# One wait for four PSUM banks becomes four waits, one at each head's first matmul, in a fused attention and expert block

## The chip, the cores and the metric

The kernel runs on one core of a Trainium2 chip. The metric is the device time of one launch in microseconds (us). The core has five engines with an instruction queue each: TensorE (PE in the profile, with its weight loads shown as PEld), VectorE (DVE), ScalarE (ACT), GpSimd (POOL) and SyncE (SP). They are ordered by semaphores alone.

## The reference, cut to what matters

```python
# x: (8, 512, 256), 16 heads, 64 rope columns and 16 content columns each
h = _layernorm(x, axis=-1) * (1 + ca) + sa
q, k, v = ...                                  # low-rank projections, rope on q_r and k_r
attn = jnp.einsum('bhqd,bhkd->bhqk', q, k) * SCALE
attn = jax.nn.softmax((attn + causal_mask).astype(jnp.float32), axis=-1)
x = x + ga * (einsum('bhqk,bhkd->bhqd', attn, v) @ w_out.T)
h = _layernorm(x, axis=-1) * (1 + cb) + sb
x = x + gb * routed_experts(h)                 # 8 merged experts, silu(gate) * up, down
```

The change touches how `attn` is computed: the raw scores, and the row maxima that the softmax subtracts.

## The kernel before, in words

The eight batch entries are eight blocks of work, one after the other. In this text block 0 is the first and block 7 the last. Each engine gets the same list of steps (`SETUP_ORDER`, `BODY_ORDER`, `LAST_ORDER`), written out by hand, and picks its part of each step. Block 0 is unrolled, blocks 1 to 6 are one loop (`Fori`), block 7 is unrolled with its own list. In the loop, the value that a semaphore is waited for depends on the block, so it has to be computed in a register first; outside it, it is a constant. A step is named by its kind and its indices: `score.021` is the kind `score` for this block (first digit 0; 1 would be the next block), head group 2, piece 1.

There are 16 heads in 4 groups of 4. A group's head h lies on partitions 32h to 32h+31, so that the four heads' matmuls use four separate row strips of TensorE. For each group there are three `maxima` steps and three `score` steps, each a quad of four PSUM banks, one for each head:

- `maxima` (lines 1086 to 1109): one matmul for each head that adds the causal mask (L1095, all 128 rows, 128 or 256 columns), and then three parts (L1104), each with one or two matmuls for each head. VectorE then takes the row maxima bank by bank (`reduce`, L863), and each of its banks is free (`max_read`) when its head is reduced.
- `score` (lines 1114 to 1128): eight parts (L1124), each with one or two matmuls for each head, the heads innermost. ScalarE then takes exponentials bank by bank (`exp`, L672), which frees the bank (`exp_ready`).

All other TensorE results take one bank: `rope` (L981 to L983, rotated by VectorE at L839), `qcon` and `kcon`, `gate`, `up`, and so on. There are seven banks, `ring0` to `ring6`, used in turn: a step's bank is the one that was used seven places earlier, and its first matmul has to wait until that earlier use has been read. `last_use` names the semaphore and the value. `take_banks` (line 387) gathers the waits of several banks, and `wait_latest` keeps for each semaphore only the highest value:

```python
def take_banks(e, b, part, steps, also=()):
    used = [last_use(b, part, step) for step in steps]
    ...
    wait_latest(e, b, [u for u in used if ...] + list(also))
    return [bank(part, PLACES[part][0][step]) for step in steps]
```

A quad calls it once, for its four banks and for its operands (`q_hi`, `rope_hi` and `k_ready` for the first `maxima` of a group; `rope_lo` and `shifted` for the first `score`). What waits there are is put on the instructions that follow: the last on the quad's first weight load, those before it on register instructions, or on instructions that do nothing else.

The other steps that the text speaks of: `value` (L1140) multiplies the exponentials with the values into the eighth bank `av`; `mix` (L1153) is the output projection, `mixed` its residual on VectorE; `qcon_hi` (L664) and `kcon_lo` (L845) make the halves of the content columns; `join` (L966, L969) ends a block on VectorE.

Of the kernel before, what the change touches and what calls it, by code (L numbers as in the profile page):

```python
# [21 lines left out]
HG = 4  # L22
# [142 lines left out]
def block_program(nc, x, wu_t, w_dq, wk_t, wdkv_t, wuk_t, wuv_t, wo_p, gw_t, gup_t, dn_t, groups, chosen,  # L165
# [3 lines left out]
    with ctx:  # L169
# [103 lines left out]
        k_ready = Count(sem("k_ready"), NG)  # L273
        q_lo = Count(sem("q_lo"), NG)
        max_read = Count(sem("max_read"), NG * NMAX * HG)
        shifted = Count(sem("shifted"), NG)
# [27 lines left out]
        waits_passed = sem("waits_passed")  # L304
# [94 lines left out]
        def wait_latest(e, b, wanted):  # L399

            latest = {}
            for count, ahead, k in wanted:
                name = id(count)
                if name not in latest or (ahead, k) > latest[name][1:]:
                    latest[name] = (count, ahead, k)
            for count, ahead, k in latest.values():
                wait(e, count, b, ahead, k)

        def take_banks(e, b, part, steps, also=()):

            used = [last_use(b, part, step) for step in steps]
            for u in used:
                if u in SETUP_READ:
                    e.wait_ge(*SETUP_READ[u])
            wait_latest(e, b, [u for u in used if u is not None and u not in SETUP_READ] + list(also))
            return [bank(part, PLACES[part][0][step]) for step in steps]

        def take_bank(e, b, part, step, also=()):
            return take_banks(e, b, part, [step], also)[0]
# [556 lines left out]
        def _(pe):  # L976
# [26 lines left out]
            def program(pe, b, part, steps):  # L1003
                for step in steps:
# [80 lines left out]
                    elif kind == "maxima":  # L1085


                        g, i = step[2:]
                        places = take_banks(pe, b, part, [(*step, h) for h in range(HG)],
                                            [(q_hi, ahead, g), (rope_hi, ahead, 2 * g + 1), (k_ready, ahead, g)] if i == 0 else ())  # L1090
                        first, span = MAX_JOBS[i][0], MAX_JOBS[i][-1][1] + (MAX_JOBS[i][-1][0] + 1) * P
                        diagonal = slice(first[1] + first[0] * P, span)
                        own = [P, (diagonal.stop - diagonal.start) // P, P]
                        for h in range(HG):
                            pe.matmul(places[h][:, diagonal].rearrange("p (n k) -> p n k", k=P), ident_b[:, :],  # L1095
                                      mask_qk[:, :].unsqueeze(1).broadcast_to(own), start=True, stop=False,
                                      skip_group_check=True)
# [15 lines left out]
                        last.then_inc(full_sem, 1)  # L1113
                    elif kind == "score":
                        g, n = step[2:]
                        places = take_banks(pe, b, part, [(*step, h) for h in range(HG)],
                                            [(rope_lo, ahead, 2 * g + 1), (shifted, ahead, g)] if n == 0 else ())
                        for p, parts_of in enumerate(SCORE_PARTS):
                            k, q = heads_of(g, *parts_of)
                            for j, q0, w, at in ST_JOBS[n]:  # L1120
                                done = p == len(SCORE_PARTS) - 1 and at == ST_JOBS[n][-1][3]
                                for h in range(HG):
                                    head = slice(h * HR, (h + 1) * HR)
                                    last = pe.matmul(places[h][:, at:at + w], k[head, j * P:(j + 1) * P], q[head, q0:q0 + w],  # L1124
                                                     start=p == 0 and at == 0, stop=done, skip_group_check=True)
                                    if done:
                                        last.then_inc(full_sem, 1)
# [129 lines left out]
```

## Time and profile before

| | |
|---|---|
| time, median of 3 runs | 1102.49 us (1101.96 to 1103.27) |
| profiled execution, its own time | 1101.17 us |
| its span | 1099.2 us |
| mean granted TensorE clock | 0.98 of full speed |
| TensorE busy | 1016.1 us, 92% of the span |
| VectorE, ScalarE, GpSimd busy | 770.1, 401.3 and 412.8 us |

The span runs from the first to the last instruction; the time of an execution has 2.0 us around it. Busy time is the share in which at least one instruction runs. An idle stretch of an engine is put down to the instruction whose semaphore ended it, and "issue" is time in which the engine waited for nothing that the profile shows.

### The profile page before, as it was taken

To read this page: it belongs to the slowest core of one execution; us is meant where nothing else is said; L and a number is where in the kernel's file an instruction comes from. 1 tells how busy PE (TensorE), PEld (TensorE's weight loads), DVE (VectorE), ACT (ScalarE), POOL (GpSimd) and SP (SyncE) were. 2 spreads that over 40 slices of the span, in tenths; PEclk is the share of its full clock that TensorE was granted. 3 is DMA by queue.
4 is the path that set the end of the run, shared out by engine and by line. 5 is a ranking of instruction groups with operands and counts; after the bars stand their busy time and mean duration, and the time that the engine had idled before them with its cause. 6 is when DMAs were issued, how large, how long until landed. Compare 5 with 4: busy or idle time off the path is not lost.

```text
span 1099.2 us, 24746 instructions
## 1 busy us (share of the span) xinstructions
PE 1016.1 (92%) x9744; PEld 723.9 (66%) x9744; DVE 770.1 (70%) x1516; ACT 401.3 (37%) x723; POOL 412.8 (38%) x349
## 2 busy tenths in 40 slices
PE   6979989999899989999899998999999998999678
PEld 4546667766676667766677666766677766776456
DVE  6767687585957868677785859678686777857344
ACT  4335433254314443145331543144431453314310
POOL 1526342264505353154422635054430544326100
PEclk9989989999999999999999999999999999999969
DMA  6220000200002000200002000020002000010000
GB/s 190 58 88 2 3 1 1 68 2 2 1 4 66 2 1 1 69 2 2 1 1 69 2 2 1 2 69 2 1 1 68 2 2 1 1 49 2 2 1 20
DMA packets 22233, 23.59 MB, mean 21 GB/s; under 512 B 6315, under 2 KB 20139, under 8 KB 22131
## 3 DMA queue, kind: packets, MB, share of 16 engines
q1 hardware_dynamic: 22130, 22.02, 6.6%
q8 instruction: 90, 1.47, 0.6%
q14 instruction: 13, 0.10, 0.0%
HBM read 17.80 MB, written 4.21 MB: 20 GB/s over the span
## 4 chain that ended last, share of the span: by engine, by line
PE 78%; DVE 7%; issue 7%; POOL 4%; ACT 2%; DMA 1%; DVEq 0%; POOLq 0%; SPq 0%; ACTq 0%
PE ring L1124 17%; PE ring L981 12%; PE ring L982 10%; PE ring L983 10%; PE ring L1196 8%; PE av L1140 6%; PE ring L1104 6%; PE ring L1095 2%; DVE mcol L863 2%; PE ring L1112 1%; PE ring L1185 1%; PE ring L1042 1%; ACT pt L672 1%; POOL rows L553 1%; POOL prod L547 1%
## 5 line engine op out<-in xcount | busy, mean ns | idle before, releaser
L672 ACT ACTIVATE pt<-ring 128x384 f32<-128x384 f32 (+1 forms) x384 | 170.8, 531 | 329.6 <-PE ring L1124 293.4
L562 POOL TENSOR_SCALAR_AFFINE_SELECT pt<-pt 128x512 f32<-128x512 f32 x128 | 79.7, 638 | 413.1 <-ACT pt L672 413.1
L863 DVE TENSOR_REDUCE mcol<-ring 128x1 f32<-128x128 f32 (+3 forms) x512 | 212.2, 481 | 19.3 <-PE ring L1104 17.8
L839 DVE TENSOR_TENSOR prod<-ring,table 128x1024 f32<-128x1024 f32 x128 | 155.3, 1217 | 97.7 <-PE ring L983 97.0
L1124 PE MATMUL ring<-rows 32*128 32x512 f32 (+3 forms) x3072 | 165.4, 329 | 18.4 <-ACT pt L672 8.5
L553 POOL TENSOR_TENSOR rows<-prod,rows 128x1024 fp32r<-128x1024 f32 x64 | 152.6, 2394 | 36.7 <-ACT rows L652 36.7
L1124 PEld LDWEIGHTS ring<-rows 32*128 32x128 f32 x3072 | 120.0, 185 | 69.4 <-issue 33.1
L546 POOL TENSOR_TENSOR prod<-prod 128x512 f32<-128x512 f32 x64 | 82.6, 1290 | 134.8 <-DVE prod L839 134.4
L652 ACT ACTIVATE rows<-prod 128x1024 fp32r<-128x1024 f32 x64 | 67.1, 1061 | 60.3 <-PE ring L1124 39.3
L1140 PE MATMUL av<-pt,vals 128*17 128x512 f32 (+3 forms) x1024 | 84.7, 436 | 3.3 <-POOL pt L562 3.2
L1196 PE MATMUL ring<-dn,pt 128*128 128x256 f32 x384 | 85.0, 381 | 0.0
L547 POOL TENSOR_TENSOR prod<-prod 128x512 f32<-128x512 f32 x64 | 84.9, 1326 | 0.0
L981 PE MATMUL ring<-h_hi,wq_lo 128*128 128x512 f32 x192 | 83.4, 434 | 1.5 <-DVE wq_lo L785 1.5
L1196 PEld LDWEIGHTS ring<-dn,pt 128*128 128x128 f32 x384 | 72.3, 190 | 12.4 <-DVE pt L954 2.2
L981 PE MATMUL ring<-h_hi,gu_lo 128*128 128x512 f32 x192 | 79.7, 415 | 0.7 <-DVE prod L839 0.7
L982 PE MATMUL ring<-h_lo,wq_hi 128*128 128x512 f32 x192 | 76.3, 398 | 0.0
L983 PE MATMUL ring<-h_hi,wq_hi 128*128 128x512 f32 x192 | 76.2, 397 | 0.0
L982 PE MATMUL ring<-h_lo,gu_hi 128*128 128x512 f32 x192 | 76.2, 397 | 0.0
L983 PE MATMUL ring<-h_hi,gu_hi 128*128 128x512 f32 x192 | 76.1, 396 | 0.0
L1124 PE MATMUL ring<-cont 32*128 32x512 f32 (+3 forms) x1024 | 75.9, 319 | 0.0
L1095 PE MATMUL ring<-mask_qk,ident_b 128*128 128x128 bf16 (+1 forms) x384 | 44.9, 239 | 25.8 <-DVE mcol L863 11.2
L1104 PE MATMUL ring<-rows 32*128 32x512 f32 (+3 forms) x1024 | 66.2, 353 | 0.0
(162 smaller groups left out, 1609.2 us busy)
## 6 DMA issues: line engine op xcount, KB each, us to landing
xn<-x_dram SPq DMA_DIRECT2D x8, 512.0 KB, 4.0
xr<-x_dram SPq DMA_DIRECT2D x8, 512.0 KB, 3.7
out_dram<-xr SPq DMA_DIRECT2D x8, 512.0 KB, 3.2
gate_bc<-gates_scratch SPq DMA_DIRECT2D x8, 256.0 KB, 4.9
pt<-wmod_dram SPq DMA_DIRECT2D x1, 1536.0 KB, 6.5
pt<-gup_t_dram SPq DMA_DIRECT2D x16, 96.0 KB, 2.6
dn<-wu_t_dram SPq DMA_DIRECT2D x1, 640.0 KB, 10.1
xr<-wk_t_dram SPq DMA_DIRECT2D x1, 512.0 KB, 8.2
```

What stands on the lines that cost most here:

```text
L547: pool.tensor_tensor(two[:, 0, :], two[:, 0, :], one[:, 1, :], ALU.add).then_inc(combined.sem, 1)
L553: pool.tensor_tensor(rows[:, par, t, 1, :, :], two, rows[:, par, t, 0, :, :].bitcast(F32), ALU.subtract)\
L672: sc.activation(pt[:, PT_AT[n] + h * w:PT_AT[n] + (h + 1) * w], ps[:, 0:w], ACT.Exp, scale=SCALE).then_inc(exp_ready.sem, 1)
L839: ve.tensor_tensor(prod[:, s % PROD, :, :], ps[:, :].unsqueeze(1).broadcast_to([P, 2, S]), table[:, :, :], ALU.mult).then_inc(rotated.sem, 1)
L863: last = ve.reduce_max(mcol[:, q, h * HR + HD:h * HR + HD + 1], ps[:, at:at + (q + 1) * P], AX_X)
L981: pe.matmul(ps, wlo(c), xhi(c), start=c == 0, stop=False)
L982: pe.matmul(ps, whi(c), xlo(c), start=False, stop=False)
L983: last = pe.matmul(ps, whi(c), xhi(c), start=False, stop=c == EC - 1)
L1104: last = pe.matmul(places[h][:, at:at + (t + 1) * P], q[head, t * P:(t + 1) * P], k[head, 0:(t + 1) * P], start=False, stop=done, skip_gro ...
L1124: last = pe.matmul(places[h][:, at:at + w], k[head, j * P:(j + 1) * P], q[head, q0:q0 + w], start=p == 0 and at == 0, stop=done, skip_grou ...
L1140: last = pe.matmul(av[HR * h:HR * h + VW, q0:q0 + w], vals[:, j, g % 2, (g // 2) * HG + h, :], pt[:, own:own + w], start=j == 0, stop=j == ...
L1196: last = pe.matmul(ps[:, t * E:(t + 1) * E], inner[:, k, tok:tok + P], dn[:, k, :], start=k == 0 and t == 0, stop=k == FT - 1 and t == 1)
```

## The change

A quad no longer takes its four banks at once. The operands' waits, where there are any, come first, on an instruction that also counts up a semaphore nobody waits for. Then each head's bank is waited for right ahead of that head's own first matmul: the mask matmul in `maxima`, the first matmul of part 0 in `score`. The matmuls, their order, the banks and the other engines' programs are as before. From here on a line number above 1090 means the kernel before; in the changed kernel the same lines stand 3 to 7 lines further down (L1095 is L1098, L1104 is L1107, L1124 is L1131, L1140 is L1147).

```diff
@@ maxima
                         g, i = step[2:]
-                        places = take_banks(pe, b, part, [(*step, h) for h in range(HG)],
-                                            [(q_hi, ahead, g), (rope_hi, ahead, 2 * g + 1), (k_ready, ahead, g)] if i == 0 else ())
+                        places = []
+                        if i == 0:
+                            wait_latest(pe, b, [(q_hi, ahead, g), (rope_hi, ahead, 2 * g + 1), (k_ready, ahead, g)])
+                            pe.sem_inc(waits_passed, 1)
...
                         for h in range(HG):
+                            places.append(take_bank(pe, b, part, (*step, h)))
                             pe.matmul(places[h][:, diagonal].rearrange("p (n k) -> p n k", k=P), ident_b[:, :],
@@ score
                         g, n = step[2:]
-                        places = take_banks(pe, b, part, [(*step, h) for h in range(HG)],
-                                            [(rope_lo, ahead, 2 * g + 1), (shifted, ahead, g)] if n == 0 else ())
+                        places = []
+                        if n == 0:
+                            wait_latest(pe, b, [(rope_lo, ahead, 2 * g + 1), (shifted, ahead, g)])
+                            pe.sem_inc(waits_passed, 1)
...
                                 for h in range(HG):
                                     head = slice(h * HR, (h + 1) * HR)
+                                    if p == 0 and at == 0:
+                                        places.append(take_bank(pe, b, part, (*step, h)))
                                     last = pe.matmul(places[h][:, at:at + w], k[head, j * P:(j + 1) * P], q[head, q0:q0 + w],
```

What this does to TensorE's queue shows at three places of the loop. The first is `score.000`, the first score quad of a block (its four banks are `ring1` to `ring4`; `down_gated` and `max_read` free them, `rope_lo` and `shifted` tell of its operands). Before:

```order
L347 REGISTER_ALU
L347 ISA [waits down_gated]
L347 REGISTER_ALU [waits max_read]
L347 REGISTER_ALU [waits rope_lo]
L1124 MATMUL ring1<-rows 128x512 [waits shifted]
L1124 MATMUL ring2<-rows 128x512
L1124 MATMUL ring3<-rows 128x512
L1124 MATMUL ring4<-rows 128x512
```

And changed:

```order
L347 REGISTER_ALU
L347 REGISTER_ALU [waits rope_lo]
L347 ISA [waits shifted]
L1131 MATMUL ring1<-rows 128x512 [waits down_gated]
L1131 MATMUL ring2<-rows 128x512 [waits down_gated]
L347 ISA
L1131 MATMUL ring3<-rows 128x512 [waits max_read]
L347 REGISTER_ALU
L1131 MATMUL ring4<-rows 128x512 [waits max_read]
```

The wait for the last bank moved from three instructions ahead of the quad to the fourth head's own matmul, and two register instructions now stand between the heads. The second place is `maxima.101`, the second maxima quad of the next block's group 0. Its fourth bank, `ring3`, is the one that the quad just ahead of it used first. Before:

```order
L347 REGISTER_ALU [waits q_lo,vals_ready,mix_gated]
L1095 MATMUL ring0<-mask_qk,ident_b 128x128 [waits max_read]
L1095 MATMUL ring1<-mask_qk,ident_b 128x128
L1095 MATMUL ring2<-mask_qk,ident_b 128x128
L1095 MATMUL ring3<-mask_qk,ident_b 128x128
```

And changed:

```order
L1098 MATMUL ring0<-mask_qk,ident_b 128x128 [waits mix_gated]
L1098 MATMUL ring1<-mask_qk,ident_b 128x128 [waits vals_ready]
L1098 MATMUL ring2<-mask_qk,ident_b 128x128 [waits q_lo]
L347 REGISTER_ALU
L1098 MATMUL ring3<-mask_qk,ident_b 128x128 [waits max_read]
```

Three of the four mask matmuls now stand ahead of the wait for `max_read`. The third place is `maxima.030`, which waits for an operand, `k_ready`, and not for a bank. Before:

```order
L347 REGISTER_ALU [waits q_hi,k_ready,max_read]
L1095 MATMUL ring4<-mask_qk,ident_b 128x128 [waits rope_hi]
L1095 MATMUL ring5<-mask_qk,ident_b 128x128
L1095 MATMUL ring6<-mask_qk,ident_b 128x128
L1095 MATMUL ring0<-mask_qk,ident_b 128x128
```

And changed:

```order
L347 REGISTER_ALU [waits q_hi]
L347 REGISTER_ALU [waits rope_hi,k_ready]
L1098 MATMUL ring4<-mask_qk,ident_b 128x128 [waits max_read]
L347 REGISTER_ALU
L1098 MATMUL ring5<-mask_qk,ident_b 128x128 [waits max_read]
L1098 MATMUL ring6<-mask_qk,ident_b 128x128 [waits max_read]
L1098 MATMUL ring0<-mask_qk,ident_b 128x128 [waits k_ready]
```

Here the wait that comes late stays ahead of the quad, and one register instruction came between the first two heads. In the whole pass of the loop, 45 register instructions now stand between the heads of its 24 quads, where none stood before; the register instructions of the whole pass grew only from 96 to 110, since fewer stand ahead of the quads.

## Rows read from the trace of the kernel before

**Rows 1.** The page: span and busy time; the chain that ended last, by engine.
```profile
span 1099.2 us, 24746 instructions
...
PE 1016.1 (92%) x9744; PEld 723.9 (66%) x9744; DVE 770.1 (70%) x1516; ACT 401.3 (37%) x723; POOL 412.8 (38%) x349
...
PE 78%; DVE 7%; issue 7%; POOL 4%; ACT 2%; DMA 1%; DVEq 0%; POOLq 0%; SPq 0%; ACTq 0%
```
**Rows 2.** Waits of TensorE in block 1 (199 to 327 us): total, times, longest.
```profile
PE ring L1095 <- DVE mcol L863: 1.5, 1, 1.5
...
PE ring L1095 <- ACT cont L664: 0.9, 1, 0.9
PE ring L1124 <- ACT pt L672: 0.8, 1, 0.8
PE ring L1124 <- DVE mcol L863: 0.7, 1, 0.7
PE ring L1095 <- issue: 0.4, 1, 0.4
```
**Rows 3.** Timeline, start of block 2: start, length, instructions [idle before].
```profile
327.41 0.39 PE L1095 MATMUL ring<-mask_qk,ident_b 128*128 128x128 bf16 x4 [0.40 <-issue]
327.73 0.74 PE L1104 MATMUL ring<-rows 32*128 32x512 f32 x8
...
329.89 0.40 PE L983 MATMUL ring<-h_hi,wk_hi 128*128 128x512 f32 x1
330.64 0.74 PE L1124 MATMUL ring<-rows 32*128 32x512 f32 x8 [0.35 <-DVE mcol L863]
```
**Rows 4.** Timeline of a quad that waits for nothing, `score.001`, block 2.
```profile
336.52 0.39 PE L983 MATMUL ring<-h_hi,wq_hi 128*128 128x512 f32 x1
336.83 0.45 PE L1124 MATMUL ring<-rows 32*128 32x384 f32 x4
```
**Rows 5.** Chain at `score.000`, blocks 2 and 0: start, length, what.
```profile
330.43 0.21 issue
...
68.96 0.24 issue
```
**Rows 6.** Chain at `score.020` of block 0, at `score.021` of block 2.
```profile
113.09 0.25 issue
...
374.64 0.14 issue
```
**Rows 7.** Chain at `maxima.101`, block 2.
```profile
411.61 0.70 DVE mcol L863
412.32 0.04 issue
```
**Rows 8.** Timeline at `maxima.101`, block 2.
```profile
412.36 0.40 PE L1095 MATMUL ring<-mask_qk,ident_b 128*128 128x128 bf16 x4 [1.55 <-DVE mcol L863]
412.69 0.45 PE L1104 MATMUL ring<-rows 32*128 32x384 f32 x4
```
**Rows 9.** A mask matmul: least, median, most ns; first and last start.
```profile
L1095 PE MATMUL ring<-mask_qk,ident_b x384: 216/219/314, 45.0 to 1022.4; 128*128 128x128 bf16 x128, 128*128 128x256 bf16 x64
```
**Rows 10.** Timeline at the first `gate` step, block 1.
```profile
295.16 0.50 PE L981 MATMUL ring<-h_hi,gu_lo 128*128 128x512 f32 x1 [0.25 <-DVE prod L839]
```
**Rows 11.** Timeline at `maxima.031`, block 7.
```profile
1020.03 0.40 PE L1095 MATMUL ring<-mask_qk,ident_b 128*128 128x128 bf16 x4 [0.68 <-ACT pt L672]
```
**Rows 12.** Blocks 2, 3, 5 and blocks 1, 4, 6, by windows: block 2 with its clock, sums.
```profile
327.41:456.41 129.00, 123.55 (x1211) 0.99 0.05 16
sum 386.89, PE 370.85; mean PE 123.62
...
sum 384.13, PE 366.81; mean PE 122.27
```
**Rows 13.** TensorE's register instructions at L347, from 330.4 and from 330.7 us.
```profile
L347 PEldq ALU_OP  x2: 32/34/36, 330.5 to 330.6; - x2
L347 PEldq ALU_OP  x2: 32/32/32, 331.0 to 331.2; - x2
```

## Prediction

> **What bounds the kernel now.** I read the page first. TensorE is busy 92% of the span and holds 78% of the chain that ended last; 7% of that chain is "issue", time in which an engine waits for nothing that the profile shows [rows 1]. So the only thing to win here is TensorE's idle time at the quads, and the reader is to look for what ends it. The waits of block 1 show how little that is: two idle stretches ahead of score quads (0.8 us ended by an exponential, 0.7 us by a reduction), three ahead of maxima quads (1.5 us by a reduction, 0.9 us by ScalarE's `cont`, 0.4 us by issue) [rows 2]. The same places come back in every block, since the order is fixed. The other quads of a block start without a stall: in `score.001` the first matmul follows the last of the step ahead by 0.31 us [rows 4], the price of going over to four row strips. A wait that ends before its turn costs nothing, so splitting it there gains nothing.
>
> The sum is made for the profiled execution, which took 1101.17 us (span 1099.2 us and 2.0 us around it). That is 1.3 us under the median of the runs, 1102.49 us; I take the gain found in it off the median. A measurement of this kernel can tell about 0.2% from no change, which is 2.2 us.
>
> **What a split wait can save in a score quad.** The heads are innermost, so behind the fourth head's first matmul stand the second matmuls of all heads. If the fourth bank is late, the first three heads get one matmul ahead each and then stand. They run beside the fourth in their own strips, so the quad ends with the fourth head's chain of eight parts, which starts at the same release as before. What is left to save is the time from the release to the matmul. The chain shows it: 0.21 us at `score.000` in block 2 and 0.24 us in block 0 [rows 5], 0.25 us at `score.020` in block 0 and 0.14 us at `score.021` [rows 6]. Where the late wait sits on the matmul itself it is 0.04 us [rows 7]. The difference is the instructions that stand between them: before `score.000`'s matmul two register instructions start at 330.5 and 330.6 us, after the release at 330.43 us [rows 5, 13], about 0.09 us for each. The change puts the late wait on the fourth head's own matmul, so I take 0.04 to 0.05 us for all. Bounds: nothing at the least, if the matmul is slow to start for another reason; at the most the whole idle stretch of rows 2, which no reason allows, as the fourth head's bank is not free sooner. I take the lag of rows 7, the same situation on the same engine.
>
> - `score.000`: 0.17 us in each of blocks 1 to 6, 0.20 in block 0, 0.05 in block 7 (constant values, fewer instructions in between, estimate): **1.27 us**.
> - `score.021`: its fourth bank is `score.020`'s first, late by construction. 0.14 − 0.05 = 0.09 us, eight blocks: **0.72 us**.
> - `score.020` in block 0: 0.20 us. `score.012` in blocks 0 and 7 and `maxima.032` in block 0 stall a little in the same way, 0.24 us together (estimate, from the 0.09 us above): **0.44 us**.
>
> **What it can save in a maxima quad.** Here the first matmul of each head is the mask, over all 128 rows, so the four run one after another. One takes 0.22 us [rows 9] and the four 0.40 us, so they follow each other by 0.06 us; the first of the three parts starts 0.33 us after the first mask [rows 8]. With three masks ahead of the wait, 0.33 − 3 × 0.06 = 0.15 us is left after the release, a saving of 0.18 us.
>
> - `maxima.101` stalls for 1.5 us in every block, for `max_read` on its fourth bank alone [rows 2, 8]. But in block 1 TensorE idles 0.25 us for VectorE at the first `gate` step, some 11 us later [rows 10], and between the two VectorE has no idle time that TensorE could shorten. There an earlier `maxima.101` only makes that wait longer: 0. In blocks 0, 2, 3 and 5 the clock falls to half right after this quad, TensorE is the later one, and 0.18 us counts, with 0.09 us of lag besides in block 0: **0.80 us**.
> - `maxima.031` in block 7 waits for its fourth bank alone for 0.68 us [rows 11]: **0.18 us**.
> - `maxima.020` loses about 0.08 us in four blocks to the instructions ahead of it. Half of it is likely given back at the next VectorE wait; I take 0.03 each: **0.12 us**.
>
> **What the change adds.** A register instruction in front of a head's matmul. Where TensorE's instruction stream is ahead of its matmuls, it is hidden: in `score.000` two such instructions of later steps ran at 331.0 and 331.2 us, while the quad had barely begun [rows 3, 13]. The cover fails where the stream comes late itself. At `maxima.030`, idle for 0.4 us "by issue" [rows 2], the late one is an operand, whose wait stays ahead of all heads. One register instruction (0.09 us) now comes between the first two masks, of which 0.06 us is covered by the mask; with the second it costs between 0.02 and 0.09 us. I take 0.05 us in six blocks: **−0.30 us**. This rests on the rows: an instruction starts only when the one ahead of it has passed its wait. The Trainium skill, "Perfetto Trace Analysis", under "Tensor Engine Instruction", says that a matmul is pushed into a wait queue and the sequencer goes on to decode the next while it waits. By that rule the inserted instruction would be worked off meanwhile and the sum would be 3.5 us instead of 3.2; the trace does not show such a case clearly, so I stay with the rows. At `maxima.100` the added step lies before VectorE's reduction, which starts late by its own queue, so it is free; at `maxima.010` the same holds, since `reduce.010` waits for VectorE's own turn of the loop. If that cover were gone, each would cost up to 0.1 us in six blocks. No DMA and no other engine's queue is touched. The setup's three maxima quads could win 0.2 us each, but there other engines are the later ones: 0, at most 0.4 us in all.
>
> Sum: 1.27 + 0.72 + 0.44 + 0.80 + 0.18 + 0.12 − 0.30 = 3.2 us, so 1101.17 becomes 1097.9 us and the median 1102.49 becomes **1099.3 us**.
>
> **Rivals.**
>
> 1. *The gain is absorbed by later waits.* TensorE reaches a VectorE or ScalarE wait 0.17 us earlier and waits there instead, as at the `gate` step of block 1 [rows 10]. Then what `score.000` and `maxima.101` save is lost and the terms for `score.021` and half of the small ones remain: about 1.1 us, 1101.4 us. Against it: in most places these engines wait for TensorE, and the releases move with it.
> 2. *The clock decides.* In blocks 2, 3 and 5 the clock falls to half for a few microseconds after the stall, in blocks 1, 4 and 6 it does not. The three with the fall took 386.89 us together, the three without 384.13 us [rows 12], so one fall costs 0.9 us. A shift of a few tenths may bring one more or one fewer: 1098.4 or 1100.2 us. Where both come together, with rival 1, this makes 1102.3 us.
> 3. *Slower: the register instructions are exposed.* There are 45 of them between heads in a pass of the loop, 270 in six passes. If a waiting matmul could not be passed by the stream, each would cost the 0.09 us of rows 13. It decides from the point where more than 35 of the 270 are exposed (3.2 / 0.09); with one in three it is 8.1 − 3.2 = 4.9 us more, 1107.4 us. The Trainium skill, "Advanced Engine Details and Errata", under "Network/Comms", gives 50 to 100 ns for reading a semaphore from the sequencer, a cost that the three added waits of each quad would have too. Against it: single-bank steps have had a register instruction and a wait on their first matmul all along, and `score.001` starts with the 0.31 us of a plain switch behind one [rows 4].
> 4. *The change does not do what it says.* The order of the instructions shows that it does; the chance is nil.
>
> **How the numbers follow.** My forecast 0.60, rival 1 0.25, rival 2 beyond its 0.9 us 0.08, rival 3 0.07. The predicted time is the forecast's, 1099.3 us. Its own range is 1097.6 us (the setup's 0.4 us, no cost at `maxima.030`, one fall fewer) to 1100.3 us (one fall more). The range that should hold 8 in 10 reaches over rival 1 and stops before rival 3: 1097.4 to 1101.9 us. Faster by more than 0.2% means under 1100.3 us: the forecast and a part of rival 2, 0.61. Within 0.2%: rival 1 and the rest of rival 2, 0.32. Slower: rival 3, 0.07.
>
> **What the profile of the changed kernel would show.** At `score.000` and `score.021`, the first three heads' matmuls well ahead of the fourth's, and 0.04 to 0.05 us between release and the fourth, with the idle stretch moved behind them. At `maxima.101`, the parts 0.15 us after the release instead of 0.33. At `maxima.030`, masks spread over 0.2 to 0.27 us instead of 0.18. Blocks 1 to 6 shorter by 0.2 to 0.4 us each. I would be wrong if the quads that start without a stall took longer than before (rival 3), or if the idle time ahead of the `gate` step, `mix` or `score.012` grew by what the quads lost (rival 1).

## Result and the profile after

The changed kernel takes 1096.33 us (median of 4 runs, 1094.83 to 1096.97) against 1102.49 us: a ratio of 0.9944, 95% interval 0.9928 to 0.9960. It is 6.2 us faster, where the prediction said 3.2 us, and the time lies below the range that was given. The sign was right, the size was half.

The page of the changed kernel: header, busy time and the chain that ended last, the same three lines as [rows 1]:

```profile
span 1095.0 us, 24777 instructions
...
PE 1026.2 (94%) x9744; PEld 730.9 (67%) x9744; DVE 771.5 (70%) x1516; ACT 401.1 (37%) x723; POOL 412.7 (38%) x349
...
PE 82%; DVE 11%; issue 4%; ACT 2%; POOL 1%; DMA 1%; POOLq 0%; DVEq 0%; SPq 0%; ACTq 0%
```

"Issue" fell from 7% to 4% of the chain, which is the lag that was to go. TensorE's busy time rose by 10 us without more work: the first matmuls of a quad now start early and are then counted beside the idle time that they cut in two. So busy time says nothing of the gain here.

The waits of block 1 (198.2 to 325.8 us), TensorE:

```profile
PE ring L1098 <- ACT cont L664: 1.0, 1, 1.0
PE ring L1098 <- DVE mcol L863: 0.9, 1, 0.9
...
PE ring L1131 <- ACT pt L672: 0.6, 1, 0.6
PE ring L1098 <- issue: 0.4, 1, 0.4
PE ring L981 <- DVE prod L839: 0.3, 1, 0.3
```

Beside [rows 2]: the wait at `maxima.101` is 0.9 us instead of 1.5, since 0.6 us of it is covered by three masks; the wait for `cont` (`maxima.100`) is longer by 0.1 us; the wait for `prod` at the `gate` step is still there.

The start of block 2 in the timeline, where `score.000` stands:

```profile
325.81 0.65 PE L1098 MATMUL ring<-mask_qk,ident_b 128*128 128x128 bf16 x4
326.39 0.74 PE L1107 MATMUL ring<-rows 32*128 32x512 f32 x8
...
328.88 1.07 PE L1131 MATMUL ring<-rows 32*128 32x512 f32 x8
329.56 0.41 PE L1131 MATMUL ring<-cont 32*128 32x512 f32 x3
329.79 0.39 PE L1131 MATMUL ring<-rows 32*128 32x512 f32 x1
329.79 0.38 PE L1131 MATMUL ring<-cont 32*128 32x512 f32 x1
```

Against [rows 3], `score.000` starts without a stall, and three heads are one part ahead of the fourth: three matmuls on `cont` at 329.56 us, the fourth's 0.23 us later. That gap between the heads stays to the end of the quad, and the forecast gave it no worth.

The same place, block 2, in the chain of waits (370.0 to 375.3 us) of the changed kernel, then of the kernel before, which shows `score.020`, the exponential of its first head, the release, and `score.021`:

```profile
370.27 2.21 PE ring L1131 x29
372.48 0.02 issue
372.51 0.61 ACT pt L672
373.11 0.04 issue
373.15 1.66 PE ring L1131 x26
```
```profile
371.82 2.19 PE ring L1124 x31
374.01 0.02 issue
374.03 0.61 ACT pt L672
```

[Rows 6] go on from there: 0.14 us from the release at 374.64 us to the first matmul. It is now 0.04 us, as predicted.

The table gives what all later readings rest on. It cuts each of blocks 1 to 6 in two: the **tail stretch**, from the last matmul's start in `score.021` to the first `gate` matmul, holds `maxima.100` and `maxima.101`; the **rest** is everything else in the block. Times are means over the six blocks of one profiled execution, worked out from the matmuls' starts.

| kernel | rest, us | against before | tail stretch, us | falls of the clock in the six tails |
|---|---|---|---|---|
| before | 80.86 | | 47.64 | 3 short |
| changed | 80.46 | −0.40 | 47.53 | 3 short |

The forecast for the rest was −0.23 us a block (0.17 + 0.09 + 0.02 − 0.05).

### The profile page after: what moved, and what is told of

Its sections match the earlier page's. It is cut to its first block, busy times and chain, and to the rows that moved or that the text cites. A ratio compares the mean times of both kernels' runs of the same rounds, so it can differ in the third digit from the quotient of the medians.

```text
span 1095.0 us, 24777 instructions
## 1 busy us (share of the span) xinstructions
PE 1026.2 (94%) x9744; PEld 730.9 (67%) x9744; DVE 771.5 (70%) x1516; ACT 401.1 (37%) x723; POOL 412.7 (38%) x349
## 4 chain that ended last, share of the span: by engine, by line
PE 82%; DVE 11%; issue 4%; ACT 2%; POOL 1%; DMA 1%; POOLq 0%; DVEq 0%; SPq 0%; ACTq 0%
PE ring L1131 17%; PE ring L981 12%; PE ring L982 10%; PE ring L983 10%; PE ring L1203 8%; PE av L1147 7%; PE ring L1107 6%; PE ring L1098 3%; DVE mcol L863 2%; DVE xr L902 1%; PE ring L1115 1%; PE ring L1192 1%; DVE prod L839 1%; PE av L1160 1%; PE ring L1042 1%
## 5 line engine op out<-in xcount | busy, mean ns | idle before, releaser
L1131 PE MATMUL ring<-rows 32*128 32x512 f32 (+3 forms) x3072 | 175.9, 330 | 9.4 <-ACT pt L672 4.9
L1131 PEld LDWEIGHTS ring<-rows 32*128 32x128 f32 x3072 | 130.4, 184 | 60.6 <-issue 35.0
L1147 PE MATMUL av<-pt,vals 128*17 128x512 f32 (+3 forms) x1024 | 85.3, 439 | 3.2 <-POOL pt L562 3.2
L1131 PE MATMUL ring<-cont 32*128 32x512 f32 (+3 forms) x1024 | 85.6, 319 | 0.0
L1098 PE MATMUL ring<-mask_qk,ident_b 128*128 128x128 bf16 (+1 forms) x384 | 49.6, 240 | 20.8 <-ACT cont L664 6.9
L1107 PE MATMUL ring<-rows 32*128 32x512 f32 (+3 forms) x1024 | 67.0, 356 | 0.0
```

The source lines that it names most:

```text
L1107: last = pe.matmul(places[h][:, at:at + (t + 1) * P], q[head, t * P:(t + 1) * P], k[head, 0:(t + 1) * P], start=False, stop=done, skip_gro ...
L1147: last = pe.matmul(av[HR * h:HR * h + VW, q0:q0 + w], vals[:, j, g % 2, (g // 2) * HG + h, :], pt[:, own:own + w], start=j == 0, stop=j == ...
```

## Experiments

Each kernel was timed against the kernel before on the same chip; the ratios are with their 95% intervals. The diffs of 1, 4, 6, 8 and 12 are against the changed kernel, those of 2, 3 and 5 against the kernel before (3: its score quads as changed). "Clock" is the mean granted clock of TensorE over a run, one number for each run. Beside the experiments stand 57 runs of the kernel before, with a clock of 0.975 to 0.982, median 0.978; 15 runs at 0.980 took 1101.6 us on average and 8 runs at 0.975 took 1104.8 us.

**1. The score quads alone.** Score quads as changed, maxima quads as before.

```diff
 elif kind == "maxima":
+    places = take_banks(pe, b, part, [(*step, h) for h in range(HG)],
+                        [(q_hi, ahead, g), (rope_hi, ahead, 2 * g + 1), (k_ready, ahead, g)] if i == 0 else ())
...
     for h in range(HG):
-        places.append(take_bank(pe, b, part, (*step, h)))
```

> Score quads as in the changed kernel, maxima quads as before. Theory A (lag: all that is won in a score quad is the time from the release of the fourth bank to the fourth head's first matmul, 0.09 to 0.21 us a quad): 2.4 us less than the kernel before. Theory B (early heads: the first three heads also end a part ahead of the fourth, 0.17 to 0.22 us, so the exponentials that read them and the bank that the next late quad waits for come earlier): 3.5 to 4.5 us less. Theory C (the surplus over the forecast lies in the maxima quads): at most 2.4 us less, and the split of the maxima quads alone gives 3 us or more.

Measured: median 1106.15 us, but from 1095.38 to 1110.22 us over 12 runs; ratio 1.0021 (0.9991 to 1.0051). The clock goes from 0.981 (1095.4 us) down to 0.965 (1110.2 us). No theory had this. Its profiled execution, of 1095.38 us at 0.981, is the fastest of the twelve; in it the rest of a block is 0.50 us shorter than before, where A counts 0.26 (0.17 + 0.09). So where the clock is the same B holds, and the clock takes the gain away in most runs.

**2. The lag alone.** In a score quad no head goes ahead.

```diff
-places = take_banks(pe, b, part, [(*step, h) for h in range(HG)],
+places = take_banks(pe, b, part, [(*step, h) for h in range(HG - 1)],
                     [(rope_lo, ahead, 2 * g + 1), (shifted, ahead, g)] if n == 0 else ())
+pe.sem_inc(waits_passed, 1)
+places.append(take_bank(pe, b, part, (*step, HG - 1)))
...
-for h in range(HG):
+for h in (HG - 1, *range(HG - 1)) if p == 0 and at == 0 else range(HG):
```

> No head ahead of another: in a score quad the waits of three banks come first, the fourth bank's wait sits on the fourth head's first matmul, and that matmul is the first of the quad. The lag goes, the early heads don't come. Theory A: the same as the split of the score quads alone, to 0.3 us. Theory B: 0.8 to 1.5 us less of a gain than that, some 2.4 us under the kernel before. In both, release to first matmul is 0.05 us at score.000 (0.21 before) and at score.021 (0.14 before).

Measured: 1102.51 us (1098.92 to 1103.80), ratio 1.0000 (0.9988 to 1.0012), clock 0.975 to 0.979. The chain at `score.000` in block 2 and from `score.020` to `score.021`:

```profile
332.74 0.69 DVE mcol L863
333.43 0.04 issue
333.47 0.73 PE ring L1126 x4
```
```profile
374.54 0.13 issue
374.67 2.22 PE ring L1126 x30
376.89 0.02 issue
376.92 0.61 ACT pt L672
377.52 0.04 issue
```

The lag is 0.04 us at both places that the text named, and the rest of a block is 0.25 us shorter, as A counts it (0.26). The other 0.25 us of the first experiment need the split. Some 0.1 us of that is this kernel's own loss: at `score.020` the added instruction keeps the lag at 0.13 us and the quad starts 0.05 us later than before. About 0.1 us at `score.021` is the early heads: measured from the last matmul of the step ahead of `score.021` to its own last, the quad gains 0.17 us with the split and 0.06 us without. The chains show 0.07 us of it: the first exponential of `score.020` starts 2.21 us (374.03 − 371.82) after the fourth head's first matmul in the kernel before, and 2.14 us after it in the changed one (372.51 against 370.37, from the matmul's start). B holds, and is small. Like the first, the kernel wins nothing in the median: its clock is lower than before.

**3. A longer lead.** The first three heads issue one part more (`score.000`) or three more (`score.021`) ahead of the fourth head; maxima quads as before.

```diff
+LEAD = {(0, 0): 1, (2, 1): 3}
...
+jobs = [(p, *job) for p in range(len(SCORE_PARTS)) for job in ST_JOBS[n]]
+ahead_of_last = LEAD.get((g, n), 0)
+for turn in range(len(jobs) + ahead_of_last):
+    for h in range(HG):
+        m = turn - (ahead_of_last if h == HG - 1 else 0)
```

> Score quads split as in the changed kernel, and at score.000 the first three heads issue one more part, at score.021 three more parts, ahead of the fourth head's first matmul. Both quads must still end eight parts of the fourth head after its release. Theory A: the same as the split of the score quads alone, to 0.3 us. Theory B: the readers of three heads start 0.2 us (score.000) and 0.5 us (score.021) earlier, and where the next release hangs on them the gain grows by 1 to 4 us over eight blocks.

Measured: 1110.17 us (1105.80 to 1111.78), ratio 1.0060 (1.0036 to 1.0083), clock 0.961 to 0.967: slower. The rest of a block is 80.32 us, 0.54 less than before and only 0.04 less than with the plain split: no late bank hangs on the heads that `score.021` finishes early. B in its strong form is wrong. All of the loss lies in the tail, 49.40 us a block. The tails of blocks 1 to 6 from `maxima.100`'s first matmul on, by windows (us, PE busy, granted clock, DMA):

```profile
281.52:297.64 16.12, 14.58 (x98) 0.79 0.00 1
411.43:427.46 16.03, 14.47 (x98) 0.79 0.00 1
541.21:557.20 15.99, 14.44 (x98) 0.79 0.00 1
670.95:686.93 15.98, 14.43 (x98) 0.79 0.00 1
800.68:816.63 15.95, 14.40 (x98) 0.79 0.00 1
930.40:946.36 15.96, 14.41 (x98) 0.79 0.01 1
```

The same stretches of the kernel before:

```profile
281.52:295.16 13.64, 11.86 (x98) 1.00 0.00 1
409.53:424.30 14.77, 13.22 (x98) 0.88 0.01 1
538.59:553.39 14.80, 13.26 (x98) 0.88 0.01 1
667.66:681.32 13.66, 11.88 (x99) 1.00 0.01 1
795.68:810.45 14.77, 13.22 (x98) 0.88 0.01 1
924.69:938.35 13.66, 11.89 (x99) 1.00 0.01 1
```

This is the plainest view of the case. The same 98 matmuls take 13.66 us at the full clock (2.4 GHz), 14.8 us with a short fall to half in it (0.88) and 16.0 us with a long one (0.79). In these tails the falls begin between 2.1 and 4.3 us behind `maxima.100`'s first matmul; `maxima.101` begins at 2.8 us, so they begin in or right behind TensorE's idle time ahead of it. That idle time is the same in all of them, 1.53 to 1.55 us, with a fall or without, so its length alone doesn't decide. A fall costs 1.1 or 2.3 us, and how many of the seven tails have one, and how long, decides more than the change does.

**4. The maxima quads alone.** The other half of the change: score quads as before.

```diff
 elif kind == "score":
+    places = take_banks(pe, b, part, [(*step, h) for h in range(HG)],
+                        [(rope_lo, ahead, 2 * g + 1), (shifted, ahead, g)] if n == 0 else ())
...
-                if p == 0 and at == 0:
-                    places.append(take_bank(pe, b, part, (*step, h)))
```

> Maxima quads as in the changed kernel, score quads as before. Theories A and B: 0.8 to 1.3 us less than the kernel before, most of it at maxima.101 (0.18 us a block, where it counts). Theory C: 3 us or more less. If the added register instructions cost more than they win (maxima.030, maxima.010, maxima.100, 0.1 us each in six blocks): 0 to 1 us more than before.

Measured: 1099.16 us (1097.09 to 1100.48), ratio 0.9968 (0.9956 to 0.9979), clock 0.981 to 0.986. The rest of a block is 80.91 us, 0.05 more than before: the split costs 0.1 us at `maxima.030` and wins about half of it back behind it. The gain is the clock's: it is higher than before in nearly all runs, and the rest of a block is no shorter. In the profiled execution it comes from block 0, whose tail had a long fall before (16.01 us from `maxima.100` on) and has none here (13.69 us); the six other tails have one short and one long fall and take 47.62 us, as before.

**5. `maxima.101` alone.** The kernel before, with the split at this one place.

```diff
+alone = (ahead, g, i) == (1, 0, 1)
-places = take_banks(pe, b, part, [(*step, h) for h in range(HG)],
+places = [] if alone else take_banks(pe, b, part, [(*step, h) for h in range(HG)],
...
 for h in range(HG):
+    if alone:
+        places.append(take_bank(pe, b, part, (*step, h)))
```

> The kernel before with the split at one place, maxima.101. Theory D (the stretch around maxima.101 decides how often the clock falls to half; the masks issued into its idle time make a fall rarer): mean granted clock 0.981 or more, and with it 1098 to 1100 us. Against it (the other maxima quads or the length of a block decide): clock as in the kernel before, 0.975 to 0.980, and 1101 us, at most 1 us less than before (0.16 us a block).

Measured: 1097.71 us (1096.53 to 1098.78), ratio 0.9953 (0.9939 to 0.9966), clock 0.984 to 0.987. Two of its tails, blocks 2 and 5, both with a fall in the kernel before:

```profile
408.92:422.59 13.67, 12.32 (x99) 1.00 0.01 1
...
793.09:806.75 13.66, 12.33 (x99) 1.00 0.00 1
```

None of the six has a fall; block 0's tail keeps its long one (15.68 us at 0.78). Where there was none before, the tail takes as long as before (13.66 us): the quad ends 0.17 us earlier, and that is given back. The prediction had it given back at the first `gate` step, but the idle time there is what it was (0.25 us in block 1, now 0.26). It goes in the middle of `logits`, whose fourth matmul starts 0.38 us behind the third instead of 0.23 (block 4); in the program that is the one that waits for `lo_ready`. So at a full clock this edit is worth nothing, and by way of the clock nearly 5 us. What D expected came: this one split raises the clock.

**6. All but `maxima.101`.** The changed kernel with the joint wait put back there.

```diff
+if (ahead, g, i) == (1, 0, 1):
+    places = take_banks(pe, b, part, [(*step, h) for h in range(HG)])
 for h in range(HG):
-    places.append(take_bank(pe, b, part, (*step, h)))
+    if len(places) < HG:
+        places.append(take_bank(pe, b, part, (*step, h)))
```

> The changed kernel with the joint wait put back at maxima.101 alone. Theory D: as the split of the score quads alone, runs between 1095 and 1110 us at a clock between 0.981 and 0.965, median over 1100 us. Against it: 1096.5 us at a clock of 0.979 or more, like the changed kernel with 0.16 us a block given back.

Measured: 1101.33 us (1099.17 to 1104.34), ratio 0.9986 (0.9975 to 0.9998), clock 0.970 to 0.977. The rest of a block is as in the changed kernel (80.47 us), the tail is 48.42 us against 47.53. As D expected, the clock is lower, though the runs don't spread as far as with the score quads alone. Without this one split, 1.1 of the changed kernel's 6.2 us are left.

**7. The changed kernel with the lead** of experiment 3.

> The changed kernel, and the first three heads one part ahead at score.000 and three at score.021. Theory B (early heads are read earlier) with theory D: 2.7 us less than the changed kernel at the same clock, so 1093 us at 0.980. Theory B without D (the falls come from the shorter block, not from the wait at maxima.101): clock 0.962 and 1108 to 1110 us, as with the lead on the score quads alone. Theory A (lag only): 1096 us.

Measured: 1093.95 us (1091.96 to 1097.67), ratio 0.9926 (0.9908 to 0.9944), clock 0.979 to 0.985. The same lead that made experiment 3 the slowest kernel does no harm once the maxima quads are split too. The expectation was wrong in its size at one clock: at 0.981 it took 1095.9 us, no less than the changed kernel (1094.8 us), and the rest of a block is 80.48 us in both (80.46). What it wins, it wins by the clock. In its profiled execution block 0's tail has no fall.

**8. The lead, and a lead at `maxima.101`:** three heads issue masks and products ahead of the fourth's mask.

```diff
+sets = [range(HG - 1), [HG - 1]] if (ahead, g, i) == (1, 0, 1) else [range(HG)]
+for heads in sets:
+    for h in heads:
+        mask(h)
+    products(heads)
```

> As the one with the lead, and at maxima.101 the first three heads issue their masks and all their products before the fourth head's mask. Theories B and D: the idle time there shrinks further, VectorE starts on three heads over 1 us earlier, clock 0.981 or more, 1091 to 1093 us. If VectorE's queue there is bound by something else: the same as the kernel with the lead alone, 1093 us. If three strips at a time are worth no more to the clock than the masks: clock as in the kernel with the lead alone.

Measured: 1092.24 us (1091.42 to 1094.38), ratio 0.9908 (0.9894 to 0.9922), clock 0.984 to 0.987, no fall in any of the seven tails.

**9. The changed kernel again,** without an edit.

> The changed kernel once more, with as many runs as the others have, to see its time beside its clock. Theory D: clock 0.978 to 0.983, between the kernels with the joint wait at maxima.101 and the one in which the fourth head is left behind altogether; 1094.5 to 1097.5 us. If the four runs so far were luck: runs at a clock of 0.970 or less, as with the score quads split alone.

Measured: 1096.36 us (1094.83 to 1097.80), ratio 0.9936 (0.9922 to 0.9949), clock 0.978 to 0.981. The first result stands.

**10. Score quads and `maxima.101`,** the other maxima quads as before: the score quads of the change, with the maxima edit of 5.

> Score quads split, and of the maxima quads maxima.101 alone; all others wait for four banks at once. From the trace: the split of the other maxima quads costs 0.1 us at maxima.030 and wins 0.05 us at score.020 and maxima.020, and moves the falls of the clock only by chance. Expected 0.3 us a block less than the changed kernel from score.000's end to score.021's end, in all 1094 to 1096 us. If the other maxima quads' masks matter for the clock too: a clock under 0.978 and over 1097 us.

Measured: 1096.11 us (1094.23 to 1097.03), ratio 0.9934 (0.9921 to 0.9948), clock 0.979 to 0.983. The rest of a block is 80.37 us, 0.10 less than in the changed kernel; the expected 0.3 us was too much. In the time it can't be told from the changed kernel. It bears on theory D, though. `maxima.101` and the tail of block 1:

```profile
283.18 0.23 PE L1098 MATMUL ring<-mask_qk,ident_b 128*128 128x128 bf16 x1 [0.20 <-DVE cont L851]
284.29 0.29 PE L1098 MATMUL ring<-mask_qk,ident_b 128*128 128x128 bf16 x1 [0.88 <-DVE mcol L863]
```
```profile
281.46:295.97 14.51, 13.42 (x98) 0.88 0.01 1
```

The idle time is broken into the same pieces as in experiment 5 (0.19 and 0.88 us in block 1), yet blocks 1, 3 and 5 have a short fall and block 0 a long one. The two kernels differ in the score quads alone. So the pieces of the idle time don't decide by themselves either.

**11. The same, with the lead at `maxima.101`** (the diff of 8 on the kernel of 10).

> As the one before, and at maxima.101 the first three heads issue masks and all products ahead of the fourth head. The lead in the score quads won nothing in the stretches without a fall, so this should give what both leads gave: clock 0.984 or more, no fall behind maxima.101, and 0.1 us a block less for the joint waits at the other maxima quads: 1091 to 1092.5 us. If the lead in the score quads is what made that kernel's clock: 1094 to 1096 us.

Measured: 1091.16 us (1088.96 to 1091.34), ratio 0.9886 (0.9871 to 0.9902), clock 0.987 to 0.990: the fastest, 1.1% under the kernel before. `maxima.100` and `maxima.101` in block 2, timeline:

```profile
405.04 0.39 PE L1098 MATMUL ring<-mask_qk,ident_b 128*128 128x128 bf16 x4 [0.87 <-ACT cont L664]
...
406.26 0.28 PE L1098 MATMUL ring<-mask_qk,ident_b 128*128 128x128 bf16 x2
406.77 0.23 PE L1098 MATMUL ring<-mask_qk,ident_b 128*128 128x128 bf16 x1 [0.22 <-DVE cont L851]
406.93 0.62 PE L1109 MATMUL ring<-rows 32*128 32x384 f32 x6
407.39 0.34 PE L1109 MATMUL ring<-cont 32*128 32x384 f32 x3
407.88 0.23 PE L1098 MATMUL ring<-mask_qk,ident_b 128*128 128x128 bf16 x1 [0.16 <-DVE mcol L863]
```

Of the 1.55 us of idle time of [rows 8], 0.22 and 0.16 us are left, in two pieces, and none of the seven tails has a fall. The work in them isn't needed sooner: the tail takes the 13.66 us that it takes at full clock in every kernel with joint waits elsewhere. What it buys is that the clock stays up.

**12. The operand waits last,** on the first head's matmul, without the instruction that carried them.

```diff
-if i == 0:
-    wait_latest(pe, b, [(q_hi, ahead, g), (rope_hi, ahead, 2 * g + 1), (k_ready, ahead, g)])
-    pe.sem_inc(waits_passed, 1)
...
-    places.append(take_bank(pe, b, part, (*step, h)))
+    places.append(take_bank(pe, b, part, (*step, h),
+                            [(q_hi, ahead, g), (rope_hi, ahead, 2 * g + 1), (k_ready, ahead, g)]
+                            if i == 0 and h == 0 else ()))
```

> The changed kernel with the operand waits on the first head's matmul, behind its bank's, and without the instruction that carried them. Theory E (the register instruction for the first bank, which now comes after the operand's release, is what makes maxima.030 and maxima.100 start later): the idle time ahead of maxima.030 is 0.04 us shorter and ahead of maxima.100 0.13 us shorter than in the changed kernel, the time from the end of score.000 to the end of score.021 0.05 to 0.1 us shorter, 0.3 to 0.6 us in all. If the instructions are worked off beside the wait: no difference in these stretches.

Measured: 1095.39 us (1093.31 to 1101.51), ratio 0.9938 (0.9918 to 0.9959), clock 0.971 to 0.984. In the trace the idle time ahead of `maxima.030` is 0.085 us shorter than in the changed kernel, that ahead of `maxima.100` 0.13 us, and from `score.000`'s end to `score.021`'s end 0.07 us are won. The expectation was right for `maxima.100` and half the size at `maxima.030`. Instructions behind the operand's wait were exposed, as theory E says; whether the register instruction alone was, or also the one that carried the waits, this edit doesn't tell, since it moves the first and takes away the second. The time is the changed kernel's within its interval.

The table of the two parts of a block, with the granted clock from `maxima.100` to the first `gate` step (0.88 is a short fall, 0.78 or 0.79 a long one). Each row is one profiled execution; the number of falls differs between the executions of one kernel too, as the clocks of the runs show. The kernel before has 3 at 0.88 and, in block 0, 0.79; the changed kernel 3 at 0.88 and, in block 0, 0.88.

| kernel | rest, us | against before | tail, us | clock in the six tails | block 0's tail |
|---|---|---|---|---|---|
| score quads (1) | 80.36 | −0.50 | 47.63 | 3 at 0.88 | 0.88 |
| lag alone (2) | 80.61 | −0.25 | 48.07 | 3 at 0.88, 1 at 0.79 | 0.79 |
| lead, joint at `maxima.101` (3) | 80.32 | −0.54 | 49.40 | 6 at 0.79 | 0.88 |
| maxima quads (4) | 80.91 | +0.05 | 47.62 | 1 at 0.88, 1 at 0.78 | 1.00 |
| `maxima.101` alone (5) | 80.90 | +0.04 | 47.09 | all 1.00 | 0.78 |
| all but `maxima.101` (6) | 80.47 | −0.39 | 48.42 | 1 at 0.88, 3 at 0.78 to 0.79 | 0.88 |
| changed and lead (7) | 80.48 | −0.38 | 47.54 | 3 at 0.88 | 1.00 |
| both leads (8) | 80.53 | −0.33 | 47.06 | all 1.00 | 1.00 |
| score quads and `maxima.101` (10) | 80.37 | −0.49 | 47.52 | 3 at 0.88 | 0.78 |
| fastest (11) | 80.45 | −0.41 | 47.08 | all 1.00 | 1.00 |
| operand waits last (12) | 80.41 | −0.45 | 47.38 | 2 at 0.88 | 0.88 |

## Why the prediction was half right

The sign and most of the mechanism were right; the sum of 3.2 us was too small. Between the two profiled executions 4.2 us of span are won: block 0 won 2.0 us, blocks 1 to 6 3.1, block 7 0.3, and the setup took 1.2 us longer. The forecast's terms for these were 0.9, 1.9, 0.4 and 0. The steps that failed, with what the runs showed:

1. *The release of `score.021` was taken as fixed,* and `score.020` as free of cost in blocks 1 to 6. The rest of a block won 0.40 us instead of 0.23.
2. *The setup's three maxima quads were put at 0.* From `kcon.01` to the end of the first `score.000` the changed kernel takes 0.8 us less, and 0.5 us of that is missing when the score quads alone are split (experiment 1).
3. *The clock was left to chance,* one fall more or fewer at 0.9 us each. But the two halves of the change move it, and in opposite directions. Splitting the score quads alone lowers it (0.965 to 0.981), splitting `maxima.101` alone raises it (0.984 to 0.987), and together they end at 0.978 to 0.981, about where the kernel before stood. That the forecast's size was no worse than half is in part luck: it has no term for either effect. In medians the split at `maxima.101` was worth 4.8 us alone (5), and 5.0 or 5.7 us in the changed kernel (6 beside the first result or beside 9); the term for it was 0.80 us.

Point by point:

- **`score.000`, 0.17 us a block: right.** From the `gate` step to the end of the next `score.000`, every kernel whose score quads wait in either new way takes 0.14 to 0.24 us less, the changed one 0.18. The lag alone gives it.
- **`score.021`, 0.09 us a block: the lag was right (0.14 to 0.04), the term too small.** The quad won 0.18 us. The step that failed was "the quad ends with the fourth head's chain of eight parts, which starts at the same release as before": `score.021`'s release is the reader of `score.020`'s first head, and that head now ends ahead of the fourth. I had treated the release as fixed.
- **`score.020`, 0.20 us in block 0 and nothing elsewhere: too small.** It was 0.20 us there, and about 0.06 us in each of blocks 1 to 6, where a late bank that I passed over costs a little too.
- **`maxima.030`, cost 0.05 us: twice that.** The half that was counted is there: the second mask starts 0.11 us behind the first instead of 0.06. The other half is idle time ahead of the quad, 0.45 us against 0.41, where instructions now stand behind the operand's wait; experiment 12 brings it to 0.36. By the rule of the Trainium skill that would have hidden the cost ("Perfetto Trace Analysis", "Tensor Engine Instruction") the sequencer decodes on while a matmul waits; this trace does not agree. In `maxima.101` of block 3 in the changed kernel, the fourth head's weight load stands at its wait through 0.88 us of idle time, and the next register instruction starts only 0.07 us after that load (539.29 us against 539.22), so it was not worked off meanwhile.
- **`maxima.020`, 0.03 us in four blocks:** 0.05 us in each of blocks 1 to 6.
- **`maxima.100`, no cost: right,** though the quad starts 0.13 us later. At full clock its tail still takes as long as before.
- **`maxima.101`, 0 where the clock holds and 0.18 us where it falls: right as far as the quad goes,** 0.22 us in the second kind (48.20 to 47.99 us); in the first kind it is given back at `logits`, not at `gate`. But this was the smaller part of what the split does. The clock's falls were rival 2, taken as chance shifts of "one more or one fewer" at 0.9 us each. Two things were wrong in it. A fall comes in two lengths, 3.4 and 6.8 us, and the longer one costs 2.3 us; block 0 alone shows it, before and after:

```profile
151.40:167.41 16.01, 14.49 (x98) 0.79 0.00 1
```
```profile
152.05:166.61 14.56, 13.46 (x99) 0.88 0.00 1
```

  These 1.45 us are most of what block 0 won; about 1.2 of them are the short fall in place of the long one (16.0 and 14.8 us in the kernel before), the rest is the quad. And the falls aren't chance alone: an edit at this one quad changes how many there are (experiments 5 and 6). The profile showed the place ("the clock falls to half right after this quad"), and I read it as a fact about the blocks and not about the quad.
- **The sum was made at a clock that the kernel before rarely exceeds.** Its profiled execution ran at 0.980; the median of 57 runs is 0.978, and 3.2 us lie between the runs at 0.975 and at 0.980. That execution lay 1.3 us under the median of its kernel and the changed kernel's 0.6 us over its own, which with the 4.2 us makes the 6.2 us measured. At one mean clock the gain is about 5 us (at 0.979: 1101.5 us before, 1096.6 us changed). By stretches of the two profiles with the same kind of fall it is 4.4 us: 2.4 in the rest of blocks 1 to 6, 0.7 in their tails with a fall, 0.8 from `kcon.01` to the first `score.000`, 0.2 in block 0 behind it and 0.3 in block 7.
- **The setup took 1.2 us longer** in spite of what its quads won. Up to `kcon.01` it took 44.67 us against 42.81. The five profiled executions with a fall of the clock at 25 us (3.4 us long) took 44.5 to 44.7 us up to there, the nine without it 42.5 to 43.3. That the fall is the cause isn't shown.
- The ends of the forecast's own range are 1097.7 and 1100.2 us by its terms, not 1097.6 and 1100.3.
- **Rival 1** (absorbed by later waits) holds for `maxima.101` at full clock only. **Rival 3** (register instructions exposed) is real at two quads a block, 0.10 us at `maxima.030` and 0.14 us at `maxima.100`. No other step in the rest of blocks 1 to 6 grew by more than 0.03 us.

Left open: what in a block brings a long fall, a short one or none. In each kernel the idle time at `maxima.101` is the same in every block, yet some blocks have a fall and others don't; in the changed kernel it is every second one (blocks 0, 2, 4 and 6). Experiments 1, 2, 3 and 6 show that shorter score quads with the joint wait kept at `maxima.101` make falls more frequent or longer, by the clocks of their runs. Experiments 5 and 6 show that the split at this quad makes them rarer. That it does so by breaking up the idle time is argued: it speaks for it that the kernels in which least of it is left, 8 and 11, had no fall in any tail and, with 5, the highest clocks, but the moment at which the idle time comes moved in every kernel too, and no experiment moved it alone. Breaking the idle time up isn't enough by itself either, since the changed kernel and experiment 10 still have falls.

## What to carry to other kernels

Before costing an edit in tenths of a microsecond, cut the program into its repeated stretches, read the granted clock of each, and compare stretches at the same clock; an idle time beside which the clock falls can be worth more than its own length, and small pieces of work put into it, needed or not, can be the gain. Here the falls were gone from all tails only in the two kernels in which most of that idle time was filled (8 and 11). When one of four banks comes late, ask not only when the quad ends but who reads its first head, and whether a later bank hangs on that reader. And take the runs' clocks, not only the profiled one's, as the state that a forecast starts from.

## What the hardware showed

- The same 98 matmuls took 13.66 us at a granted clock of 1.00, 14.8 us at 0.88 and 16.0 us at 0.79, with falls to half of 3.4 and 6.8 us. Over the runs of one kernel (experiment 1), 0.981 to 0.965 of clock made 14.8 us.
- Behind an idle time of TensorE of 1.5 us, the same in every block, three of six tails had a fall in the kernel before and six of six in experiment 3. In pieces of about 0.2 and 0.9 us none of six had one in experiment 5, but three of six in experiment 10. In pieces of 0.22 and 0.16 us there was none in the seven tails of experiment 11.
- Heads in their own row strips keep a gap between them over a whole quad: one that starts a part ahead (0.23 us) also ends a part ahead, without slowing the others.
- Instructions between a wait that ends late and the next matmul cost time: the idle time at `maxima.100` was 1.00 us with two instructions between that wait and the first weight load (changed), and 0.87 us with one (experiment 12, and the kernel before).
- The stream of TensorE's instructions didn't go past a weight load that stood at a wait: the next register instruction started 0.07 us after the load (`maxima.101`, block 3, changed kernel).
